# Five PSUM banks for the work units instead of four, two for the scores instead of three, and another spread of the value projections

## The reference, cut to what matters

```python
h = tokens(x); h = concatenate([h, text(x_txt)], axis=1)        # 16 x 1101 x 128
q, k, v = (einsum('bsd,hdk->bhsk', layernorm(h), w) for w in (wq, wk, wv))
o = softmax(q @ k.T / 8) @ v                                    # 8 heads of 64
h = h + einsum('bse,ed->bsd', heads(o), head_kernel)
y = layernorm(h) * scale + bias
out_shared = swiglu(y @ shared_in.T) @ shared_out.T + b
routed = sum over the 2 chosen of 8 experts of weight_e * (swiglu(y @ expert_in.T) @ expert_out[e].T)
return h + out_shared + routed
```

## Time and profile before

| | |
|---|---|
| median of 3 runs | 5187.49 us (5181.03 to 5187.82) |
| the profiled execution | 5181.64 us, its span 5179.9 us |
| busy share of the span | PE 91%, PEld 65%, DVE 62%, POOL 57%, ACT 51% |
| mean granted TensorE clock | 0.977 |
| one item of the loop | about 318 us (from 2261.4 to 2579.2 us, an item in the middle) |

### The profile page before, as it was taken

The page is one execution under the profiler, slowest core; times in us unless marked ns, Lnnn a source line. Parts: engine busy times, 40 slices in busy tenths (PEclk is TensorE's granted clock), DMA queues, the critical chain, the costliest instruction groups (busy, mean ns, idle before and its releaser), DMA issues.

```text
span 5179.9 us, 94570 instructions
## 1 busy us (share of the span) xinstructions
PE 4702.1 (91%) x25829; PEld 3377.0 (65%) x25829; DVE 3214.4 (62%) x7726; ACT 2647.0 (51%) x6408; POOL 2943.0 (57%) x1803
## 2 busy tenths in 40 slices
PE   5999989999899998999999998998999989999997
PEld 3666666666666666666666666666666666666666
DVE  5556656566565666656566565665656656566654
ACT  2664554555545545545455455455455554555542
POOL 0775555555555565565555555555555555555662
PEclk7999999999999999999999999999999999999998
DMA  1000000000000000000000000000000000000000
GB/s 39 14 21 14 12 23 13 18 14 13 23 13 18 13 18 19 13 18 19 18 14 13 18 18 17 14 13 23 13 18 14 13 23 12 18 14 13 19 9 18
DMA packets 110624, 87.00 MB, mean 17 GB/s; under 512 B 69264, under 2 KB 101895, under 8 KB 110087
## 3 DMA queue, kind: packets, MB, share of 16 engines
q1 hardware_dynamic: 110087, 80.46, 5.5%
HBM read 59.63 MB, written 19.65 MB: 15 GB/s over the span
## 4 chain that ended last, share of the span: by engine, by line
PE 69%; ACT 10%; DVE 9%; issue 6%; DMA 2%; SPq 2%; POOL 0%; ACTq 0%; DVEq 0%; POOLq 0%
PE o_ps L832 21%; PE work L729 11%; PE work L788 8%; PE scores L813 8%; PE scores L815 8%; DVE part_max L986 3%; ACT probs L929 2%; PE work L749 2%; PE work L772 2%; PE work L740 2%; PE work L723 2%; ACT k_a L881 2%; DVE h_out L1030 2%; PE work L716 1%; DMA q_b<-max_rows 1%
## 5 line engine op out<-in xcount | busy, mean ns | idle before, releaser
L1215 POOL TENSOR_TENSOR sums<-sums,probs 128x736 f32<-128x736 f32 (+3 forms) x1344 | 2365.1, 1760 | 1178.1 <-ACT probs L929 1138.6
L929 ACT ACTIVATE probs<-scores 128x368 f32<-128x368 f32 (+3 forms) x3456 | 1459.5, 474 | 1571.9 <-PE scores L815 1534.1
L986 DVE TENSOR_REDUCE part_max<-work 128x1 f32<-128x368 f32 (+3 forms) x3456 | 1650.3, 530 | 597.5 <-PE work L729 585.4
L813 PE MATMUL scores<-q_a,k_a 128*128 128x368 f32 (+3 forms) x3456 | 1174.9, 340 | 133.0 <-DMA q_b<-max_rows 72.3
L832 PE MATMUL o_ps<-probs,values 128*64 128x368 f32 (+1 forms) x6912 | 1229.5, 491 | 0.0
L815 PE MATMUL scores<-q_b,k_b 128*128 128x368 f32 (+3 forms) x3456 | 1149.6, 333 | 0.0
L729 PE MATMUL work<-k_a,q_a 128*128 128x368 f32 (+3 forms) x3456 | 973.9, 363 | 46.0 <-ACT normed L891 26.6
L729 PEld LDWEIGHTS work<-k_a,q_a 128*128 128x128 f32 (+1 forms) x3456 | 593.8, 185 | 374.9 <-issue 232.2
L832 PEld LDWEIGHTS o_ps<-probs,values 128*64 128x64 f32 (+1 forms) x6912 | 460.5, 140 | 548.3 <-issue 448.7
L813 PEld LDWEIGHTS scores<-q_a,k_a 128*128 128x128 f32 (+1 forms) x3456 | 638.4, 185 | 231.1 <-issue 104.5
L1211 POOL TENSOR_TENSOR sums<-probs 128x736 f32<-128x736 f32 (+1 forms) x192 | 338.2, 1761 | 687.9 <-ACT probs L929 683.6
(11 more groups left out here) (185 smaller groups left out, 4915.3 us busy)
## 6 DMA issues: line engine op xcount, KB each, us to landing
sums<-inverse_rows SPq DMA_DIRECT2D x384, 92.0 KB, 2.7
resid_rows<-heads_t SPq DMA_DIRECT2D x16, 576.0 KB, 3.0
h_out<-resid_rows SPq DMA_DIRECT2D x16, 576.0 KB, 3.9
heads_t<-in_pe_table_dram SPq DMA_DIRECT2D x16, 512.0 KB
out_dram<-h_out SPq DMA_DIRECT2D x16, 512.0 KB
inv_cols<-sums SPq DMA_DIRECT2D x384, 1.4 KB
inverse_rows<-inv_cols SPq DMA_DIRECT2D x192, 2.9 KB
q_b<-max_rows SPq DMA_DIRECT2D x128, 4.0 KB
```

The lines of the kernel that those rows point to most:

```text
L813: nc.tensor.matmul(o, k_a[p % 2][i][:, t * P:t * P + n], q_a[p % 2][i][:, c0:c0 + cw], start=True, stop=False)
L929: nc.scalar.activation(probs[0:n, slot(s), i, 0:cw], scores[0:n, h % SB, 0:cw], ACT.Exp, scale=DH ** -0.5).then_inc(probs_ready, 1)
L986: nc.vector.tensor_reduce(part_max[0:n, i * NT + j, c:c + 1], w[0:n, 0:keys], AX.X, ALU.max).then_inc(drained[k], 1)
L1215: nc.gpsimd.tensor_tensor(acc, acc, probs[0:n, slot(s), :, 0:cw], ALU.add).then_inc(sums_done, 1)
```

## The change

`LANES` goes from 4 to 5 and `SB` from 3 to 2. A unit now waits for the unit five places earlier, and head h of the scores for the exp of head h-2, that is of the same head in the step before. The weights with which the value projections are spread go from PE's load alone to the sum of DVE's and ACT's; the units planned after them in the same steps (`up`, `shared`, `expert`) move with them.

```diff
-LANES = 4
-SB = 3
+LANES = 5
+SB = 2
...
-EVEN_MAX, EVEN_V, EVEN_POST = (0, 1, 0), (1, 0, 0), (1, 0.5, 0)
+EVEN_MAX, EVEN_V, EVEN_POST = (0, 1, 0), (0, 1, 1), (1, 0.5, 0)
```

## The result

The changed kernel takes 4949.7 us (median of 4 runs, 4947.67 to 4958.35), the kernel before 5184.8 us beside it. The ratio is 0.955, with a 95% interval of 0.9534 to 0.9567: 235 us faster, where I forecast 5050 us (137 faster) and a range that ended at 4975. The direction and the mechanism were right; the gain came out at 1.7 times the forecast, because the term for the fifth bank took each wait of PE at its printed idle time and because less of the item ran at the lower clock.

The account below looks back on a forecast made before the run. PE, busy 91% of the span, sets the pace, its largest idle time being a shortage of unit banks. Gains 11.2 less 0.4 and 1.7 make 9.1 us per item, times 15 items 137 us: 5050 us, range 4975 to 5170.

Parts of the forecast that it names:

- The fifth bank: Unit waits throughout an item: a unit needs the drain five places back, not four; waits shrink, place by place.
- all the ceilings: Low end of the range: every upper bound comes true, plus 0.17 us at about 20 waits; near 14 us per item.
- the terms that were one long wait: Unit waits in steps 4-5, 19-20 and 35, removed by the fifth bank: 0.6, 1.5 and 1.9 us per item.
- runs of `max` units: Eight runs, steps 17 to 101: one more bank lets PE run one unit further ahead, 2.0 us per item.
- Steps 28-33 and 56-59: Stretches where ACT is busy most of the time: gains of 0.6 and 1.3 us, ceilings 3.1 and 2.2.
- Steps 23-27: Between `maxrow` in step 23 and step 27: the DMA wait takes the gains, none counted.
- The moved units: Steps 82-83 and 86 gain 1.5 us per item; the value projection leaving step 106 costs 0.36 us elsewhere.
- The second score bank: Scores need the exp of the step before: four waits grow by 0.42 us each, 1.7 us per item lost.
- The start of an item: First scores wait 4.02 us for the maxima's DMA, behind the output DMA; this hangs on step 102, not PE's later work.
- The waits came back on ACT: Rival: PE finds exps, `neg_max` and hidden tiles as late as before; half the gains go, 5135 us, chance 0.25.
- the rule that brief idling between groups pulls it down: Cited for the rival that two score banks couple PE to ACT and slow the kernel: 5210 us, chance 0.10.
- The skill's remark that PSUM double-buffering: Cited for the rival that nothing happens because data, not banks, set the waits: about 5187 us, chance 0.07.

Follow-up runs that it names:

- e3: Kernel before with two score banks in place of three, four unit banks and value projections as before: 5212.9 us, ratio 1.0057.
- e1: Kernel before with five unit banks and two score banks, value projections spread as before: 5000.3 us, ratio 0.9653.
- e2: Kernel before with only the new spread of the value projections, four unit and three score banks: 5165.1 us, ratio 0.9966.
- e4: Changed kernel with six unit banks and one score bank: 6868 us in a single run.
- e8: Changed kernel with two items per loop turn and the output DMA moved from step 102 to 105: 4922.5 us, ratio 0.9495.
- e9: e8 with seven items in the loop's body and 2 turns: 4885.3 us, ratio 0.9423.

## Why the prediction was right, and where it was wrong

- **What bounds the kernel, and the trade.** Right. The unit waits were for banks and mostly went away with one more (14.4 to 4.7 us of idle time in an item); the third score bank was worth little.
- **The step that failed** is "The fifth bank": the sum took each wait at the idle time printed in the timeline. The first part said that each wait of PE is 0.17 us longer than that, but this never entered the sum, only the low end of the range, and the 0.1 us of the first matmul behind a wait was not seen at all. The term was 9.7 us per item without the moved units; it measured 14.9 (e3 to e1). Of these 7.9 are idle time of PE, 21.8 waits fewer at 0.25 us make 5.5, and 2.7 us less at 1.2 GHz make 1.3. The clock was put at nothing: the prediction saw it fall only at the start of an item and says that elsewhere the short waits left it at 1.00, but rows 6 don't include step 35, and behind the 1.92 us of rows 3 the clock did fall, in that very item.
- **The range was added up wrongly.** With all the ceilings it names the gains are 11.2 + 0.8 + 0.9 + 2.5 + 1.6 = 17.0 us, with 0.17 us for each of 20 waits 20.4, less 2.1 it is 18.3 us per item and not 14: 4913 us and not 4975. The measured 4949.7 lies above that. So the prediction's own upper bounds, rightly added, held the result.
- **By place** the terms that were one long wait came out well: 0.6 for steps 4-6 (measured 0.6), 1.5 for 19-22 (1.4). This is in part luck, since a shorter wait stands in place of each (0.16 us in step 5, 0.40 in step 20) and takes back what the fixed price would have added. Those made of several short waits were forecast at half their size: runs of `max` units and the units around them, 1.7 for steps 62-75 against 3.3, of which 1.1 came with the moved units (e1 to after). The `expert` unit of step 35 did lose its wait on the drain of the `max` unit; in its place PE waits 0.34 us for the hidden data, as this row of the changed kernel shows:

```profile
2265.41 0.68 PE L777 MATMUL work<-down_sh,hid 128*128 128x128 f32 x4 [0.34 <-DVE hid L1018]
```

- **Steps 28-33 and 56-59**, where I held ACT for the bound and cut the gains to 0.6 and 1.3: 1.2 and 1.8 measured. ACT was nearly full in these windows, and the gain did stay under its ceiling of 3.1 and 2.2, but by less than I had allowed; that ACT is what held it is argued, not shown.
- **Steps 23-27**, where I counted none because a DMA wait would take all: 0.8. The gains ahead of step 27 were indeed taken, by the DMA wait in e3 and e1 and by a wait of 2.04 us for an exp in step 26 of the changed kernel; what the mean won is mainly 0.6 us of clock in step 27, which stays full in e3, e1 and the changed kernel.
- **The moved units.** 1.1 us per item forecast, 1.2 measured with four banks (e2), 3.5 with five. The 1.2 agrees by luck, as more time at 1.2 GHz took back some 2.6. So at equal clock this term was too small by a factor of about three in either kernel: 1.1 us of it came in steps 62-75, for which the sum had nothing from the moves.
- **The second score bank.** 1.7 us per item forecast, 1.9 measured (e3), though not place by place. The minimum of 1.0 us from step to step was borne out by step 13, whose length grew from 0.66 to 1.06 us.
- **The start of an item.** The rule that the DMA chain makes PE's work before it free was half of the truth. For the changed kernel it made no difference, as both bounds stood there.
- **The rivals.** The waits came back on ACT in part only: L813 waits 3.1 us more per item, for 9.7 us less in front of the units, and the scores' part is in the 1.9 of e3. The mean clock stayed at 0.98, but the rule that brief idling between groups pulls it down (the Trainium skill, "TensorE: Matmul & The Clock Gate", on the second failure mode) does show in this case: behind waits of 1.3 and 1.9 us in the kernel before, in about half of the items, and in e4, with its wait at each head, where the mean was 0.918. It worked in favour of the change, which took these waits away. The skill's remark that PSUM double-buffering gave the kernel measured there no further gain (same page, "HAM oscillation") has no counterpart here, where PE waited for drains: one bank more was worth 213 us.

## What to carry to other kernels

Price a wait of PE by the distance between the starts of the matmuls around it, with and without, and not by the idle time printed: here each wait cost 0.27 us more, and when there are 50 in an item of 318 us the count matters beside the sum. Then compare the time at each clock, step by step and not by the mean alone: in e2 a mean that fell only from 0.977 to 0.968 stood for some 2.6 us per item. When PSUM is divided, give each consumer the depth that its chain needs (here two banks for scores, one step's worth) and the rest to the queue with the most waits. Where two edits meet in the same steps, work out what PE runs into next: with the bank free at step 83, it waited 2.27 us for data. And where removing one wait shows nothing, look for a second one of like length beside it.

## What had not been expected of the hardware

The clock can fall behind a wait of 1.3 to 1.9 us in one item and stay full behind the same wait in the next, as the rows of steps 27, 34 and 35 above show.

The turn of the loop has a price on PE: at the start of an item inside a turn the next scores came 1.17 us behind the last (exp to exp), at the turn 4.4 to 5.2 us, with the idle time put down to "issue". From e8 to e9 five turns fewer saved 37 us, 7.5 us each, twice the 3.3 to 4.0 us that the start itself shows. Of the other half, 9 of the 37 us lie in steps 0-3, 6 in steps 23-27 and 3 in steps 36-53; why the later ones got shorter is not shown. The Trainium skill has the likely reason ("Runtime: NRT & Kernel Launch", Instruction fetch mechanics): instructions are fetched ahead in sequence, and a taken branch to a target outside the pages at hand forces a fetch before anything can go on. The runs here agree with it in time and place, but no run shows the fetch itself.
